# A sorting pass in 62 chunks: one-hots by row from spread edge fields, running tables per tile on VectorE, and one fp32 product for h

## The reference, cut to what matters

```python
h = jnp.maximum(_layernorm(x), 0.0)
head, tail, rel = h[src], h[dst], relation_emb[edge_type]
att_scores = sigmoid(concat([head, rel], -1) @ att_w + att_b)
aggr = segment_sum(att_scores * tail, src, num_segments=6250)
x = x + tanh(aggr @ W_w.T + W_b)
```

## Time and profile before

| | |
|---|---|
| median of three runs | 7741.46 us |
| the profiled execution | 7789.98 us |
| its span, first to last instruction | 7787.8 us |
| mean granted TensorE clock | 0.611 |
| sorting pass: first to 61st burst of scatters | 333.65 to 3862.42 us |
| busy over the span | TensorE 42%, VectorE 46%, ScalarE 31%, GpSimd 42% |

### The profile page before, as it was taken

The page is one execution under the profiler, slowest core; times in us unless marked ns, Lnnn a source line. Parts: engine busy times, 40 slices in busy tenths (PEclk is TensorE's granted clock), DMA queues, the critical chain, the costliest instruction groups (busy, mean ns, idle before and its releaser), DMA issues. The chain is left out here.

```text
span 7787.8 us, 93760 instructions
## 1 busy us (share of the span) xinstructions
PE 3233.5 (42%) x31759; PEld 2600.9 (33%) x31760; DVE 3605.5 (46%) x6570; ACT 2450.0 (31%) x5029; POOL 3252.3 (42%) x3386
## 2 busy tenths in 40 slices
PE   4744444444444444444457743332222223332224
PEld 3633443343343343344357621111111111111113
DVE  7744443443444444444367724444444444444443
ACT  0122222222232232232212234444444444444432
POOL 0144344444434434434450045555555555555542
PEclk9866666666666666666666655555555555555555
DMA  3011111111111111111156322222333333333310
GB/s 46 29 52 45 42 50 45 43 49 46 44 42 52 45 42 52 45 42 51 37 126 125 76 75 83 83 83 83 86 86 86 88 84 84 84 84 83 86 55 17
DMA packets 651114, 497.92 MB, mean 64 GB/s; under 512 B 556547, under 2 KB 565379, under 8 KB 651056
## 3 DMA queue, kind: packets, MB, share of 16 engines
q1 hardware_dynamic: 509120, 240.52, 12.6%
q0 software_dynamic: 108640, 196.86, 8.7%
q10 hardware_dynamic: 33296, 59.81, 2.2%
HBM read 286.61 MB, written 210.32 MB: 64 GB/s over the span
## 5 line engine op out<-in xcount | busy, mean ns | idle before, releaser
L518 POOL DMA_INDIRECT records<-rec,place x1612 | 1550.5, 962 | 2388.8 <-ACTq L637 1901.1
L1210 POOL DMA_INDIRECT got_a<-kv_table,idx_a x1612 | 1524.3, 946 | 1418.5 <-DVE idx_a L1322 914.3
L1225 PE MATMUL p_a<-ident,flat_attr 128*128 128x128 f32 x434 | 124.3, 434 | 1730.6 <-ACT attr_t L1266 965.6
L550 PE MATMUL p_h<-window,dst_hot 128*128 128x64 bf16 x4836 | 378.2, 218 | 943.4 <-issue 943.4
L725 DVE TENSOR_SCALAR dst_hot<-p_dst,number 128x512 bf16<-128x512 f32 x434 | 308.9, 712 | 972.6 <-remote 707.4
L539 PE MATMUL p_look<-parts,lo_hot_t 128*128 128x98 bf16 x4836 | 538.1, 250 | 468.3 <-DVE earlier L743 461.2
L743 DVE TENSOR_TENSOR earlier<-p_same,less_b 128x512 bf16<-128x512 f32 x434 | 282.5, 651 | 938.7 <-PE p_same L585 519.7
L610 ACT COPY h_dst<-p_h 128x256 f32<-128x256 f32 x434 | 155.0, 357 | 1770.7 <-remote 1291.6
L1225 PEld LDWEIGHTS p_a<-ident,flat_attr 128*128 128x128 f32 x434 | 75.2, 214 | 1768.9 <-ACT attr_t L1266 989.9
L1345 DVE TENSOR_TENSOR prod<-got_a,wide 128x1664 f32<-128x1664 f32 x62 | 117.0, 1887 | 1108.8 <-remote 1107.7
L550 PEld LDWEIGHTS p_h<-window,dst_hot 128*128 128x128 bf16 x4836 | 280.5, 114 | 954.2 <-issue 954.2
(11 more groups left out here) (339 smaller groups left out, 9872.4 us busy)
## 6 DMA issues: line engine op xcount, KB each, us to landing
sums<-packed_a ACTq DMA_DIRECT2D x62, 936.0 KB
q_starts<-zero_q SPq DMA_DIRECT2D x62, 884.0 KB
rec_r<-records SPq DMA_DIRECT2D x124, 442.0 KB
qin<-q_starts SPq DMA_DIRECT2D x62, 884.0 KB
attr_a<-records SPq DMA_DIRECT2D x62, 442.0 KB
records<-rec,place POOLq DMA_INDIRECT x1612
got_a<-kv_table,idx_a POOLq DMA_INDIRECT x1612
stage<-in_edge_attr SPq DMA_DIRECT2D x61, 416.0 KB
```

Source lines behind the costliest of these rows:

```text
L518: nc.gpsimd.indirect_dma_start(k.records, bass.IndirectOffsetOnAxis(ap=place[b][:, t:t + 1], axis=0), rec[b][:, t, :], None).then_inc(s_se ...
L550: last = nc.tensor.matmul(p_h[:, j * D:(j + 1) * D], dst_hot[qb][:, j * P:(j + 1) * P], window[b][:, part, :], start=(part == 0), stop=(pa ...
L1210: nc.gpsimd.indirect_dma_start(got[b][:, t, :], None, k.kv_table, bass.IndirectOffsetOnAxis(ap=idx[b][:, t:t + 1], axis=0)).then_inc(s_got ...
L1225: last = nc.tensor.transpose(p_a[:, g * P - c0:(g + 1) * P - c0], flat_attr[:, g * G:(g + 1) * G, :].rearrange("p t c -> p (t c)"), k.iden ...
```

## The change

What it does, in `setup` and `sort`:

- The edge fields lo, hi and dst (less the chunk's base) are written to DRAM as three long bf16 rows, `field_rows`, by three DMAs of SyncE with pieces of 26 values, and loaded again chunk by chunk as a tile of three partitions. A product with a constant matrix of three rows (`select`) spreads a row over all partitions: lo, 128 * hi + lo, and dst, each 512 columns wide for a group.
- The one-hot of lo by row comes from that on ScalarE, as Relu(1 - Abs(lo - partition)), in fp32. The transposes and the copy of `p_t` go.
- `earlier` compares the spread node number, to which a second product adds 16384 where the edge isn't earlier, with `src_f`. `p_same` goes.
- The tables of places (one for each of 2 x 26 tiles, fp32) are built by VectorE, one add of 49 columns a tile; the logit table lies behind them. `look` is then one fp32 product of 98 columns a tile and the bf16 product with `earlier`. The parts, `p_place`, the `hist` copies and their products go.
- h[dst] is one fp32 product a tile, with the window in fp32; the table `h3_table` of three bf16 parts and what made it go.
- `p_h` has two banks; ScalarE scales straight out of it into a buffer of its own, `h_gated`, and `assemble`, now at group 2, copies the gates and this buffer to `rec`. The wait for the scatters moves from the first `gated` to `assemble`. `place` is made on VectorE.

```diff
@@ setup, SyncE
+                sp.wait_ge(s_fields, 1)
+                    for a, field in enumerate((k.lo_b, k.hi_b, k.dst_in)):
+                        sp.dma_start(k.field_rows[a, :].rearrange("(c p t) -> p c t", p=P, t=T),
+                                     field[:].rearrange("p (c t) -> p c t", t=T)).then_inc(k.s_field_rows, 16)
                 sp.wait_ge(s_h, 1)
                 sp.dma_start(by_node(k.h_table), h[:]).then_inc(s_table, 16)
-                sp.wait_ge(s_h3, 1)
-                sp.dma_start(k.h3_table.rearrange("(h l) c -> l h c", l=P), h3[:].rearrange("p h a d -> p h (a d)")).then_inc(s_table, 16)
@@ setup, VectorE
-                c.then(nc.vector.tensor_copy(h3[:, :, 0, :], h[:]))
-                c.then(nc.vector.tensor_tensor(h_rest[:], h[:], h3[:, :, 0, :], ALU.subtract))
-                c.then(nc.vector.tensor_copy(h3[:, :, 1, :], h_rest[:]))
-                nc.vector.tensor_tensor(h3[:, :, 2, :], h_rest[:], h3[:, :, 1, :], ALU.subtract).then_inc(s_h3, 1)
-                split3(c, k.parts[0][:, :, 1, :], gate[:], gate_r[:])
@@ sort, SyncE, per chunk
+                        wait(sp, s_dst, (n - 1) * GROUPS)
+                        sp.dma_start(fields[b][:], k.field_rows[:, bass.ds(n * P * T, P * T)]).then_inc(s_fields[b], 16)
@@ sort, TensorE: look
-                        for part in range(3):
-                            nc.tensor.matmul(both, at, k.parts[qb][:, part, :, :], start=(part == 0), stop=False)
-                        for e in range(j):
-                            nc.tensor.matmul(to, at, hist[qb][:, e, :], start=False, stop=False)
-                        last = nc.tensor.matmul(to, earlier[qb][:, j, :], k.hi_hot[b][:, :, g * G + j], start=False, stop=True)
+                        nc.tensor.matmul(both, lo_hot_t[qb][:, j * P:(j + 1) * P], k.tables[:, slot:LOGIT + 1:LOGIT - slot, :], start=True, stop=False)
+                        last = nc.tensor.matmul(both[:, 0:HI], earlier[qb][:, j, :], k.hi_hot[b][:, :, g * G + j], start=False, stop=True)
...
-                    wait(pe, s_h_copied, q)
+                    wait(pe, s_gated, q - 1)
                     for j in range(size(g)):
-                        for part in range(3):
-                            last = nc.tensor.matmul(p_h[:, j * D:(j + 1) * D], dst_hot[qb][:, j * P:(j + 1) * P], window[b][:, part, :],
-                                                    start=(part == 0), stop=(part == 2))
+                        last = nc.tensor.matmul(p_h[qb][:, j * D:(j + 1) * D], dst_hot[qb][:, j * P:(j + 1) * P], window[b][:], start=True, stop=True)
@@ sort, TensorE: a group (the transposes, p_same and p_place go)
+                            wait(pe, s_lo_away, q)
+                            nc.tensor.matmul(p_lo[:, 0:m * P], k.select[:, LO, :], rows, start=True, stop=True).then_inc(s_lo, 1)
+                            wait(pe, s_earlier, q)
+                            nc.tensor.matmul(p_src[:, 0:m * P], k.select[:, NODE, :], rows, start=True, stop=False)
+                            nc.tensor.matmul(p_src[:, 0:m * P], k.identb[:], k.not_less[:, 0:m, :].rearrange("p g e -> p (g e)"), start=False, stop=True).then_inc(s_src, 1)
+                            wait(pe, s_dst_hot, q)
+                            nc.tensor.matmul(p_dst[:, 0:m * P], k.select[:, TO, :], rows, start=True, stop=True).then_inc(s_dst, 1)
+                            wait(pe, s_tables, q)
+                            for j in range(m):
                                 last = nc.tensor.matmul(p_hist[:, j * HI:(j + 1) * HI], k.lo_hot[b][:, :, t], k.hi_hot[b][:, :, t], start=True, stop=True)
@@ sort, ScalarE
+                    nc.scalar.activation(lo_away[qb][:, 0:m * P], p_lo[:, 0:m * P], ACT.Abs, bias=k.minus_number[:]).then_inc(s_lo_away, 1)
+                    nc.scalar.activation(lo_hot_t[qb][:, 0:m * P], lo_away[qb][:, 0:m * P], ACT.Relu, bias=k.ones[:, 0:1], scale=-1.0).then_inc(s_lo_hot, 1)
...
-                        nc.scalar.activation(rec[b][:, t, H0:REC], h_dst[b][:, t, :], ACT.Copy, scale=rec[b][:, t, GATE:GATE + 1])
+                        last = nc.scalar.activation(h_gated[b][:, t, :], p_h[qb][:, j * D:(j + 1) * D], ACT.Copy, scale=gate[b][:, t:t + 1])
...
+                    wait(act, s_sent[b], SCATTERED * i)
+                    nc.scalar.copy(rec[b][:, :, GATE], gate[b][:])
+                    nc.scalar.copy(rec[b][:, :, H0:REC], h_gated[b][:])
@@ sort, VectorE: a group
+                            c.mark(add(b, g, 0))
+                            v.tensor_scalar(dst_hot[qb][:, 0:m * P], p_dst[:, 0:m * P], k.number[:], None, ALU.is_equal).then_inc(s_dst_hot, 1)
+                                c.mark(add(b, g, 1))
+                            v.tensor_tensor(
+                                earlier[qb][:, 0:m, :], p_src[:, 0:m * P].rearrange("p (g e) -> p g e", e=P),
+                                bc(k.src_f[:, bass.ds(n * T + g * G, m)], 2, P), ALU.is_equal).then_inc(s_earlier, 1)
+                                c.mark(add(b, g, 2))
+                                pick(older[0] * GROUPS + older[3], older[2], older[3], qb)
+                            add(b, g, m - 1).then_inc(s_tables, 1)
+                                summed(older[0] * GROUPS + older[3], *older)
```

More of the change, by code:

```diff
@@ L444, in sort @@
         tile, bank, sem = helpers(k, ctx)
[L445 to L447 removed]
+        lo_away = [tile(f"lo_away{b}", [P, G * P], BF16) for b in range(2)]
+        lo_hot_t = [tile(f"lo_hot_t{b}", [P, G * P]) for b in range(2)]
+        dst_hot = [tile(f"dst_hot{b}", [P, G * P]) for b in range(2)]
         earlier = [tile(f"earlier{b}", [P, G, P], BF16) for b in range(2)]
[L449 to L450 removed]
+        window = [tile(f"window{b}", [P, D]) for b in range(2)]
+        fields = [tile(f"fields{b}", [3, P * T], BF16) for b in range(2)]
         picked = tile("picked", [P, G, 2, HI])
[L452 to L454 removed]
+        place_gate = [tile(f"place_gate{b}", [P, T, 2]) for b in range(2)]
+        logit = [tile(f"logit{b}", [P, T]) for b in range(2)]
+        gate = [tile(f"gate_s{b}", [P, T]) for b in range(2)]
         place = [tile(f"place{b}", [P, T], I32) for b in range(2)]
         stage = [tile(f"stage{b}", [P, T, EC]) for b in range(2)]
[L457 removed]
+        h_gated = [tile(f"h_gated{b}", [P, T, D]) for b in range(2)]
         rec = [tile(f"rec{b}", [P, T, REC]) for b in range(2)]
@@ L625, in assemble @@
+                    last.then_inc(s_gated, 1)
                 def assemble(n, i, b):
                     cols = bass.ds(n * T, T)
-                    nc.scalar.copy(place[b][:], place_all[:, cols])
+                    wait(act, s_sent[b], SCATTERED * i)
                     nc.scalar.copy(rec[b][:, :, DST], k.dst_f[:, cols])
                     nc.scalar.copy(rec[b][:, :, SRC], k.src_f[:, cols])
+                    nc.scalar.copy(rec[b][:, :, GATE], gate[b][:])
+                    act.wait_ge(s_gated, n * GROUPS + GROUPS)
@@ L642, in body @@
                         for g in range(GROUPS):
[L643 to L653 removed]
+                            lo_one_hot(n * GROUPS + g, b, g)
                             if g >= 3:
@@ L717, in body @@
                             m = size(g)
-                            older = None if at_start(i, b) and g < 2 else behind(n, i, b, g)
-                            parts = k.parts[qb][:, :, 0, :]
-                            wait(dve, s_look, q - 1)
-                            dve.wait_ge(s_placed, q + 1)
-                            c.mark(nc.vector.tensor_copy(parts[:, 0, :], p_place[:, 0:HI]))
+                            older = None if at_start(i, b) and g < 2 else behind(i, b, g)
+                            dve.wait_ge(s_hist, q + 1)
@@ L1700, in build @@
                 k.last_attr = tile("last_attr", [P, T, EC])
-                k.parts = [tile(f"parts{b}", [P, 3, 2, HI], BF16) for b in range(2)]
+                k.tables = tile("tables", [P, LOGIT + 1, HI])
                 setup(k)
```

218 lines of the change are left out of this document (98 added, 120 removed).

## The result

The changed kernel takes 8182.39 us (median of four runs, 8165.58 to 8190.66) against 7742.29: ratio 1.0563, 95% interval 1.0551 to 1.0576, 5.6% slower. Its profiled execution took 8165.58 us, with a span of 8163.6; before 7789.98 and 7787.8. Each run is read only against the kernel before beside it; single executions of that kernel beside e1 to e4 took 7780.85 us and beside e5 to e8 7739.96, so differences of some 40 us between single runs mean little.

A forecast was written before the change was run, and what follows sets the result against it. It took GpSimd's scatter burst, during which TensorE passes 92 records, plus VectorE's loop afterwards as the bound: 36.9 + 18.6 = 55.5 us a period; -198 - 16 + 4 = -210, so 7580 profiled, 7531 expected; range 7340 to 7840.

The forecast's parts named there:

- The held stretch: From a chunk's first scatter to 4.2 us after its last, TensorE completes slowly: 36.9 us, 92 records, 3.9 groups left.
- rival 1: The stretch during the scatters counts records: 3.3 groups left, period 53.2 us, time 7393; chance 0.24.
- The first group after it at half clock, 6.1, 2.9 more at 3.8: Groups after the scatters: one at half clock, 6.1 us, then 2.9 at 3.8 us each, 11.0 us.
- free stretch: Rest of a chunk's period, after the scatters: 22.2 us before, forecast 18.6 with 1.5 for `assemble`.
- the 1.5: Charge per chunk for `assemble`, its longer copy and gates on ScalarE breaking the loop: 1.5 us, 0 to 3.
- Sixteen fp32 records: A group's fp32 product records on TensorE: 3.7 us at 1.2 GHz, 2.0 at 2.4.
- streaming alone: Pricing TensorE's fp32 records by columns streamed only: a group would take 1.2 us less at half clock.
- Rival 3: TensorE becomes the bound at half clock after the scatters: period 62.2 us, time 7933; chance 0.13.
- VectorE 3.8 us: VectorE's work per group, the bound at full clock: 3.8 us against nearly 4.0 before.
- The loop without slack: lo product, two passes, sigmoid, four scalings and p_h, through TensorE and ScalarE: 3.8 us a group, no slack.
- Setup -16: In `setup`, next stage starts near 93 instead of 109.75: -16 us; +8 if writes of 52 bytes cost twice.
- The tail +4: The last chunk's longer `assemble` and tail: +4 us.

The follow-up runs named there:

- e1: Changed kernel with the spread rows put in tile order in SBUF by one GpSimd copy a chunk: 7834.86 us, beside 7780.85 for the kernel before.
- e4: Kernel before with one part of the change alone, h by one fp32 product a tile: 7958.32 us, beside 7780.85 for the kernel before.
- e5: Changed kernel with spread rows in tile order and h by one bf16 product a tile, lower 16 bits left out: 7375.89 us, beside 7739.96.
- e8: Changed kernel with tile order, 128 rows in the spread products and scatters in portions of four: 7033.00 us, beside 7739.96 for the kernel before.
- e2: Changed kernel with 128 rows in place of 3 in the spread products, the others zero: 7964.58 us, beside 7780.85 for the kernel before.
- e6: Changed kernel with GpSimd waiting for VectorE's next group before every fourth scatter: 7397.07 us, beside 7739.96 for the kernel before.
- e10: Changed kernel with tile order and portions of four scatters, spread products of 3 rows: 5901.50 us, beside 5586.24 for the kernel before.
- e12: Changed kernel with 128 rows in the spread products and portions of four scatters, stride kept: 6228.89 us, beside 5586.24 for the kernel before.
- e9: Changed kernel with tile order and 128 rows in the spread products, scatters in one burst: 5684.02 us, beside 5586.24 for the kernel before.
- e16: Changed kernel with tile order, 128 rows and portions of four scatters, same kernel as e8, timed: 7029.12 us, ratio 0.9079.
- e15: Changed kernel with its 26 scatters in two halves of 13, same kernel as e11: 7739.89 us, beside 7741.47 for the kernel before.
- e11: Changed kernel with its 26 scatters in two halves of 13: 6427.83 us, beside 5586.24 for the kernel before.
- e14: Changed kernel with tile order and 128 rows, one burst, same kernel as e9: 7712.46 us, beside 7741.47 for the kernel before.

## Why the prediction was wrong

I forecast 7531 us, range 7340 to 7840, with 0.72 for faster; it is 8182, slower, outside the range.

- **The held stretch: right in length and records.** 36.9 us and 89 to 92 records, as in the kernel before. I took 3.9 groups as left behind it; 3.3 to 3.4 are, the count of rival 1. It is no law of the chip: on one chip it wasn't there at all.
- **"The first group after it at half clock, 6.1, 2.9 more at 3.8": this is the step that failed.** Every full group that TensorE works through without a wait takes 7.95 us, so the free stretch is 27.9 us and not 18.6, and 60 periods are 558 us longer than forecast. Put into my own sum with rival 1's 3.3 groups, 36.9 + 3.3 x 7.95 + 1.5 is 64.6; measured 64.8. That it fits so well is in part luck: the 1.5 was for `assemble`, which TensorE doesn't wait for, and TensorE's idle 1.5 us there is the end of the standstill.
- Its two errors are apart. *The work at half clock* is 7.95 us, not 6.1: I priced the columns of the spread products by the clock alone, and they read one value in 52 bytes (1.32, e1) and have 3 rows beside products of 128 (0.45, e2). Together 1.77 of the 1.85 missing. Sixteen fp32 records were right: 3.9 us against 3.7. (The aside that streaming alone would make it 1.2 us less doesn't come out of its own numbers: 16 x (0.23 - 0.12) is 1.8.) *The clock* I took from the kernel before, whose records show it rising after each burst; in the changed kernel it never rises. Rival 3 had this (7933, with 0.13; its turning point is 5.2 us a group by its own sum, not 5.0), argued down by "TensorE would be busy without a pause, and in rows 8 such a run was at 1.00". e6 refutes that argument: 51.9 us of 51.9 busy, no rise. Twelve products of 128 columns aren't these.
- The Trainium skill (SBUF — State Buffer, Door 1: The DMA port swizzle) has a rule that I left out: it says that SBUF has lines of 16 bytes and each access that crosses to a new line pays; by it a stride of 52 bytes pays at every column. The traces agree, for the one stride that was run: 0.86 us against 0.40 to 0.43 for 512 columns at half clock.
- The Trainium skill (TensorE: Matmul & The Clock Gate, What's actually happening) says that a busy engine is given 2.4 GHz. e6, e10 and e12 disagree for these products: no record in the pass and durations of 1.2 GHz, with TensorE never pausing.
- **VectorE 3.8 us: right** (L665 0.200, L711 0.745, L717 0.684, L671 0.820, L679 0.561 by the lines of VectorE, all as priced), and it hides under 7.95. *ScalarE*: two passes 0.69 and 0.72, not 1.16 in sum but 1.41; hidden too. The loop without slack shows where the clock is up and no signal is late: in e9 TensorE waits some 3 us a chunk for `h_gated`, never over 2.7 at once. In e16 it waits 12 us a chunk for the same tile, up to 10.2 at once, but there ScalarE itself gets p_lo's signal late (8.5 us in the median from 20 us after the first scatter), so that isn't the loop alone.
- **Setup -16: wrong sign.** +4.6 (I had +8 as the far end). The three writes held SyncE 0.4, 12.3 and 17.8 us, 30.5 in sum, near the 27 I had; but behind them the h table held it another 17.7, where it had taken 0.40. The first burst comes 29.9 us later; 25 of it are the start of the pass at half clock, some nine groups with no scatters beside them, which my sum left out.
- **The tail +4:** +6.6 to the last burst; the 19.1 us less behind it aren't the change's, as told above.

What holds TensorE's signals back while GpSimd scatters stays open, and so does what it is in the products that keeps the clock at 1.2 GHz. Shown of the signals: the delay grows over a long burst and is gone or smaller where the burst is broken up (e6, e15), it isn't in the program alone (e9 and e11 against e14 and e15, the same kernels), and what passes goes by neither records nor groups exactly.

## What to carry to other kernels

Price a matmul by the stride of its moving operand and by what stands next to it, and at the clock of the changed instruction mix, not of the old one: a mix with products of 3 rows, or with strided ones, kept TensorE at 1.2 GHz here though it never paused (e10, e12; e6 with both). A clock column is evidence only where the trace has clock records; otherwise divide columns by time. Where one engine's long burst of small DMAs makes another's signals late, split the burst before reducing the work: four scatters at a time gave 8.5% in the kernel before and 9.5% in the changed one, for a wait before each portion. That holds on the chips where signals come late; on the one where they don't, no pair with and without portions was run, and there is no standstill to win back.

## What was not expected of the hardware

- The same program took 7741 and 5586 us on two chips, 28% apart. The kernel before has no trace on the second; e9 and e14, one kernel on both, are 2028 us apart. 184 records fall in the stretch of the sorting pass in which e14 has 85. 947 of the 2028 us lie behind the pass, where GpSimd gathers in long bursts: there ScalarE waits 950 us for late signals of the p_a products in e14, up to 45 us behind the product, and in e9 such a signal is never more than 0.4 us late. So late signals account for the part behind the pass too. From the profile of e14:

```profile
L1272 ACT COPY attr_t<-p_a 128x512 f32<-128x512 f32 x124 | 66.0, 533 | 1051.3 <-remote 950.2
```

- TensorE at half clock through 51.9 us without a pause, and so through the whole pass (e6).
- A product of 3 rows next to one of 128 costs some 0.13 us a change; a moving operand with a step of 52 bytes doubles the time of 512 columns at 1.2 GHz, from 0.40 to 0.86 us.
